# A conditioned residual kernel on one core: the stores of x are issued from GpSimd's queue instead of ScalarE's

## What is computed

```python
# _L0: W = weights[condition]; einsum('bct,bcd->bdt', x, W)
# _L1: w = weights[subjects]; b = biases[subjects]; einsum('bct,bcd->bdt', x, w) + b^T
x = x + _L0_cond_ref(x, L0_cond_weights, itok_B_0_15)
x = x + _L1_cond_ref(x, itok_B_0_31, L1_cond_weights, L1_cond_biases)
```

## Time and profile before

| | us |
|---|---|
| median of 3 runs | 642.38 |
| lowest, highest | 642.14, 642.54 |
| the profiled execution's own time | 642.87 |
| its span, first to last instruction | 641.1 |

### The profile page before, as it was taken

The page is one execution under the profiler, slowest core; times in us unless marked ns, Lnnn a source line. Parts: engine busy times, 40 slices in busy tenths (PEclk is TensorE's granted clock), DMA queues, the critical chain, the costliest instruction groups (busy, mean ns, idle before and its releaser), DMA issues.

```text
span 641.1 us, 6225 instructions
## 1 busy us (share of the span) xinstructions
PE 537.6 (84%) x2308; PEld 234.0 (37%) x2308; DVE 329.2 (51%) x259; ACT 333.2 (52%) x385; POOL 123.9 (19%) x263
## 2 busy tenths in 40 slices
PE   1899999999889888898898888988988988889870
PEld 0344444443334333343333333333433433334330
DVE  0366666665455445545554555455445544554460
ACT  0466666666455455554554555556545555555450
POOL 2222222222121121221221212212212112122000
PEclk9999999999999999999999999999999999999995
DMA  9999999999999999999999999999999999999995
GB/s 359 428 414 430 428 432 429 429 430 432 431 429 432 431 430 431 431 430 431 430 431 431 430 429 432 430 433 429 431 433 428 429 433 430 429 432 430 430 429 255
DMA packets 18931, 271.82 MB, mean 424 GB/s; under 512 B 2241, under 2 KB 2274, under 8 KB 2274
## 3 DMA queue, kind: packets, MB, share of 16 engines
q1 hardware_dynamic: 9504, 137.37, 50.4%
q10 hardware_dynamic: 9410, 134.26, 49.0%
HBM read 137.40 MB, written 134.22 MB: 424 GB/s over the span
## 4 chain that ended last, share of the span: by engine, by line
DMA 73%; PE 20%; DVE 3%; POOLq 0%; issue 0%; ACT 0%; DVEq 0%; POOL 0%; SPq 0%; ACTq 0%
DMA out_dram<-xt 42%; DMA xt<-in_x_dram 30%; PE acc L160 17%; PE acc L155 3%; DVE xt L224 2%; DMA w_sb<-in_w_dram 1%; DVE xt L226 1%; DVEq L39 0%; ACT L246 0%; POOLq L127 0%; POOLq L130 0%; POOL map0T L137 0%; POOL map L138 0%; ACT both L247 0%; ACT both L246 0%
## 5 line engine op out<-in xcount | busy, mean ns | idle before, releaser
L160 PE MATMUL acc<-xt,both 64*128 64x512 f32 x2048 | 471.7, 602 | 70.6 <-DMA xt<-in_x_dram 68.2
L251 ACT ACTIVATE xt<-acc,bias_of 64x1024 f32<-64x1024 f32 x256 | 283.6, 1108 | 272.3 <-PE acc L160 269.9
L224 DVE TENSOR_SCALAR xt<-acc,bias_of 64x1024 f32<-64x1024 f32 x128 | 163.3, 1276 | 279.8 <-PE acc L160 279.8
L160 PEld LDWEIGHTS acc<-xt,both 64*128 64x128 f32 x2048 | 189.5, 187 | 321.5 <-issue 224.1
L226 DVE TENSOR_SCALAR xt<-acc,bias_of 64x1024 f32<-64x1024 f32 x128 | 165.0, 1289 | 1.9
L137 POOL TENSOR_TENSOR map0T<-w0T_sb,ident 128x128 f32<-128x128 f32 x128 | 65.4, 511 | 467.8 <-PE acc L155 456.1
L155 PE MATMUL acc<-map,map0T 128*128 128x256 f32 x256 | 73.3, 409 | 0.9 <-POOL map L138 0.9
L138 POOL TENSOR_TENSOR map<-w_sb,ident 128x128 f32<-128x128 f32 x128 | 65.3, 510 | 0.0
L155 PEld LDWEIGHTS acc<-map,map0T 128*128 128x128 f32 x256 | 43.8, 191 | 52.3 <-issue 47.8
L247 ACT ACTIVATE both<-acc 64x256 f32<-64x256 f32 x64 | 24.2, 378 | 0.7
L246 ACT ACTIVATE both<-acc 64x256 f32<-64x256 f32 x64 | 24.1, 377 | 0.7
(11 more groups left out here) (4 smaller groups left out, 0.4 us busy)
## 6 DMA issues: line engine op xcount, KB each, us to landing
xt<-in_x_dram SPq DMA_DIRECT2D x64, 2048.0 KB, 27.0
out_dram<-xt ACTq DMA_DIRECT2D x64, 2048.0 KB, 40.5
w_sb<-in_w_dram SPq DMA_DIRECT2D x1, 2048.0 KB, 9.3
w0T_sb<-in_w0T_dram SPq DMA_DIRECT2D x1, 1024.0 KB, 4.8
cond_sb<-in_conds_dram ACTq DMA_DIRECT2D x1, 1.0 KB
bias_sb<-in_bias_dram ACTq DMA_DIRECT2D x1, 16.0 KB, 9.4
cond_rep<-in_conds_dram ACTq DMA_DIRECT2D x1, 16.0 KB, 11.1
```

Source lines behind the costliest of these rows:

```text
L160: return nc.tensor.matmul(acc[:, j * CHUNK:(j + 1) * CHUNK], both[k * HC:(k + 1) * HC, buf, u, :], xt[k * HC:(k + 1) * HC, slot, u * T + j ...
L224: nc.vector.tensor_scalar(xt[0:HC, q % SLOTS, a:a + HALF], acc0[0:HC, a:a + HALF], bias_of[0:HC, 2 * q:2 * q + 1], None, ALU.add)
L251: return nc.scalar.activation(xt[HC:C, q % SLOTS, v * T + a:v * T + a + HALF], acc1[v * HC:(v + 1) * HC, a:a + HALF], ACT.Identity, bias=b ...
```

## The change

ScalarE no longer waits for the pair's two halves and no longer issues stores. GpSimd issues all 64 stores from its own queue: the store of pair q - 3 behind the four sums of pair q, after waiting for `hi_out0` and `hi_out1` of pair q - 3; the last three behind the last sums. The final waits for the stores move to GpSimd too.

```diff
@@ -122,6 +122,11 @@
             pool.wait_ge(w0_loaded, LOAD)
             pool.wait_ge(w1_loaded, LOAD)
             GROUP = 16
+            def store(q):
+                pool.wait_ge(hi_out0, q + 1)
+                pool.wait_ge(hi_out1, q + 1)
+                pool.dma_start(out_pairs[q, :, :], xt[:, q % SLOTS, :]).then_inc(stored[q % SLOTS], LOAD)
+
             for b in range(B):
@@ -137,6 +142,12 @@
                 nc.gpsimd.tensor_tensor(map0T[:, q % 2, :, k, :], w0T_v[:, bass.ds(i0[b % GROUP], 1), :, :], ident_v, ALU.add)
                 nc.gpsimd.tensor_tensor(map1[:, q % 2, k, :, :], w1_v[:, bass.ds(i1[b % GROUP], 1), :, :], ident_v,
                                         ALU.add).then_inc(maps_ready, 1)
+                if k == 1 and q >= 3:
+                    store(q - 3)
+            for q in range(PAIRS - 3, PAIRS):
+                store(q)
+            for q in range(SLOTS):
+                pool.wait_ge(stored[q], LOAD * TURNS)
@@ -261,11 +272,6 @@
                 act.wait_ge(hi_done1, q + 1)
                 odd_out(q, 0, HALF)
                 odd_out(q, 1, HALF).then_inc(hi_out1, 1)
-                act.wait_ge(hi_out0, q + 1)
-                act.wait_ge(hi_out1, q + 1)
-                act.dma_start(out_pairs[q, :, :], xt[:, q % SLOTS, :]).then_inc(stored[q % SLOTS], LOAD)
-            for q in range(SLOTS):
-                act.wait_ge(stored[q], LOAD * TURNS)
```

## The result

The changed kernel takes 647.86 us (median of 6 runs, 647.69 to 648.70), the kernel before 642.51 in the same comparison. The ratio is 1.0082 (1.0071 to 1.0093): slower by 0.8%, 5.3 us. The profiled execution of the changed kernel takes 647.87 us with a span of 646.1, against 642.87 and 641.1.

What follows compares the result with a forecast made beforehand. The prediction took the DMA engines' transfer volume to bound the kernel, 9.75 us a pair. It summed 642.87 (the profiled execution) + 0 + 0 + 0 = 642.87, forecast 642.9, with a range of 641.0 to 650.0 us.

Steps and rivals of the forecast that it cites:

- What bounds the kernel: Steady stretch: DMA engines full at about 430 GB/s, 9.75 us of volume a pair; queueing absorbs a longer step.
- What is taken from ScalarE, 0: ScalarE loses 64 store issues, 21.6 us in total, which come out of its waiting for TensorE; gain 0.
- The sign I gave, waits grown by 20 us: If the forecast was right, ScalarE's waits for TensorE would grow by some 20 us.
- What is put on GpSimd, 0: GpSimd's sums and stores don't hold each other up; the store finds GpSimd waiting, 4.2 us early; cost 0.
- The issue: Each store's issue on GpSimd takes about 1.3 us, between 0.34 and 2.28, covered by the backlog of transfers; cost 0.
- the lock between VectorE and GpSimd: VectorE in a two-port mode could delay each GpSimd store by up to one VectorE instruction; taken as 0.
- The packets, 0: Stores' packets on the new queue take the same engine time as before; cost 0, at most 14.5 us.
- The end: At the last store issue, some 5 us of earlier stores hide a delay of 1 to 2.3 us; cost 0.
- Stores first: Rival: new queue served ahead of loads, last load lands late, end 4.9 us later; 647.5 us, chance 0.17.
- Dearer packets: Rival: store packets take 1% or so longer on each DMA engine, 3.1 us; about 646 us, chance 0.22.
- the straggler: Rival: the one DMA engine ending some 5 us late no longer does, up to 5.4 us gained; 637.5, chance 0.10.
- GpSimd as the bound: Rival: a GpSimd issue over 7.8 us, say 10, sets the pace of each pair; 770 us, chance 0.03.

Runs made afterwards that it cites:

- run 7: The changed kernel with each of GpSimd's stores split in two by columns, 128 DMAs in all: 652.70 us, ratio 1.0151.
- run 8: The changed kernel with the stores of the last eight pairs issued by ScalarE, which also waits for all stores: 646.00 us, ratio 1.0047.

## Why the prediction was right or wrong

The range of 641.0 to 650.0 held the result, and slower had 0.42. But the forecast, 642.9 and no change, was not what came, and the rival that named nearly this number named another cause. The range reached up to 650.0 for stores served first and for dearer packets, neither of which came; that it held 647.86 is luck.

- **What bounds the kernel: right.** 431 GB/s through, 9.8 us for a pair, a circuit of 78.6 us with the queueing as its elastic part. The stores grew by 2.1 us and the loads shrank by 2.5.
- **What is taken from ScalarE, 0: right.** It still waits 268.0 us for TensorE (269.9 before). The sign I gave, waits grown by 20 us, was wrong: an issue isn't counted as busy, and the row counts from the end of the last busy instruction, so the 21.6 us stood in the 269.9 already.
- **What is put on GpSimd, 0: right.** The waits ahead of its stores sum up to 294.1 us, all for VectorE: GpSimd stands ready each time, 4.43 us early in the middle of the run.
- **The issue: mis-sized, and covered as argued.** 0.57 us by the median, 0.70 at most, where I took 1.3. Doubled in run 7 it left no gap. Of the lock between VectorE and GpSimd that the prediction took from the Trainium skill (SBUF — State Buffer, "SBUF: two separate sides"), the runs show nothing in the length of an issue, which starts 0.3 us behind VectorE's last instruction and takes 0.53 to 0.70 us. The changed kernel says little on it, as VectorE stands idle during 62 of the 64 issues. Run 7 says more: there over forty issues lie inside a VectorE instruction, as the one at 58.80 beside VectorE's from 58.79 to 60.07, and all 64 second issues of a pair take 0.53 to 0.54 us. No row shows whether these VectorE instructions are in the mode that the rule asks for, nor when a store's first byte moves.
- **The packets, 0: right.** 314.0 us of engine time against 314.1.
- **The end: the step that failed.** The wrong term is "Cost 0" for the end of the program. "At the last issue some 5 us of earlier stores are still ahead of it" is right for the transfers; the wait for the last store passes 0.3 us earlier than before. The sum ended with the last landing, though. It took the 1.8 us between span and time as a constant and looked at no instruction behind the landing. The missing term is GpSimd's drain, 0.046 + 64 x 0.082 = 5.29 us. By 642.87 - 0.3 + 5.3 the sum would have been 647.9, against 647.87 measured. The trace of before could not give the price: its drain of GpSimd, at 590.7, ends at 592.4, right behind GpSimd's last sum (592.33), so its 1.68 us are the wait for that sum and no price of DMAs. It did show that such an instruction stands behind the last wait, and that was the question to ask. The last waits moved to GpSimd, and with them whatever GpSimd does when it leaves. I had listed "the final waits" in the change and costed only the stores.
- **Stores first, 0.17 for 647.5: wrong for this kernel.** Its 4.9 us agree with 5.3 by chance. Loads landed sooner, not later, and nothing was idle before the end. Its arithmetic was near: in run 8, where two store queues do crowd out the loads, the last load lands 14.8 us later and the end goes from 640.4 to 644.3, 3.9 us. The packets by which the prediction backed this rival, from the Trainium skill (DMA: Bandwidth & Descriptors, "Queues, rings and completion order"), would have shown as short stores; with one queue for loads and one for stores they took 42.6 us.
- **Dearer packets, the straggler, GpSimd as the bound: none came.** The last 5.9 us before 641.1 still have a share of 0.05, one engine alone.

## What to carry to other kernels

When work moves to another engine, follow that engine to its very last instruction: DMAs issued on GpSimd leave a bill that its drain pays at the exit, here 0.082 us for each one that had not been settled before, whatever its size. It is free if those DMAs have landed and the drain is over while other engines still work. So let another engine wait for the last transfers (that won back 2.9 of the 5.3 us here), and put the bill behind few large DMAs or DMAs that landed early. No run here kept all 64 stores on GpSimd and came back to 642.5 us. And spreading stores over a second queue in a kernel bound by its transfers is no neutral act: it takes turns from the loads, and what the loads lose shows as idle transfer engines once the last of them has landed.

## What the runs showed of the hardware that I had not expected

- GpSimd's drain takes 0.046 us behind no DMA, 0.135 behind one, 2.68 behind 32, 5.28 to 5.29 behind 64 (2 KB to 2 MB each), 10.51 behind 128 small ones, and 0.046 when an earlier drain has settled them.
- Started while the last store is in flight, it ends 2.5 us (64 stores) or 1.3 us (32) behind the point at which ScalarE sees the last landing: half of the price is paid ahead.
- 128 stores of 1 MB left a drain of only 2.35 us, with one stop of 2.32 us in front of the 114th issue, the first that takes the queue past 16,384 packets; why is open.
- GpSimd's issue of a 2 MB store takes 0.57 us of the engine, ScalarE's 0.34 us of its queue; the packets take the same time on either queue.
